# A state-space decoder layer with routed experts: router operands in PSUM, row norms on ScalarE, and evenly spread scatters and output matmuls

## The reference

```python
x = x + _L0_attn_ref(_layernorm(x, axis=-1), ...)     # state-space mixer
x = x + _L0_xattn_ref(_layernorm(x, axis=-1), ...)    # int8-quantised MLP, weights per sequence
x = x + _L0_ffn_ref(_layernorm(x, axis=-1), ...)      # 16 routed experts (top 2) and a shared one
```

```python
dA = jnp.exp(d_t[..., None] * A)
h = h * dA + (d_t * u_t)[..., None] * B_t[:, None, :]
y = jnp.einsum('bdn,bn->bd', h, C_t)
```

## Time and profile before

| | |
|---|---|
| median of 3 runs | 1877.12 us (1876.48 to 1877.83) |
| the profiled execution | 1878.76 us, its span in the trace 1876.7 us |
| busy: PE, VectorE, ScalarE, GpSimd | 1450.3, 1477.8, 762.5, 1057.5 us |
| first part, to the first scan | 0 to 118 us |
| scan stages of batch 0, 1, 2, 3 | 118 to 360, 487 to 777, 904 to 1192, 1319 to 1603 us |
| transitions | 360 to 487, 777 to 904, 1192 to 1319 us |
| `last` and the last stage | 1603 to 1680, 1680 to 1877 us |

### The profile page before, as it was taken

The page is one execution under the profiler, slowest core; times in us unless marked ns, Lnnn a source line. Parts: engine busy times, 40 slices in busy tenths (PEclk is TensorE's granted clock), DMA queues, the critical chain, the costliest instruction groups (busy, mean ns, idle before and its releaser), DMA issues.

```text
span 1876.7 us, 19131 instructions
## 1 busy us (share of the span) xinstructions
PE 1450.3 (77%) x5208; PEld 817.3 (44%) x5208; DVE 1477.8 (79%) x2381; ACT 762.5 (41%) x1296; POOL 1057.5 (56%) x643
## 2 busy tenths in 40 slices
PE   6926656998578899997669899996679998449872
PEld 2312212444344565443435565443445664237662
DVE  2269999787998999797989999788989998873111
ACT  3454344236423555237324555247324553021221
POOL 0079999403759889403859888305769987201001
PEclk9967778999689999998689999998779999768996
DMA  2360000413324674514324663624225773214884
GB/s 96 140 246 13 0 0 1 141 40 135 141 107 133 204 225 130 191 43 157 149 95 154 205 217 110 202 83 169 86 96 157 235 222 133 74 62 141 255 299 158
DMA packets 99019, 255.28 MB, mean 136 GB/s; under 512 B 11488, under 2 KB 11616, under 8 KB 93792
## 3 DMA queue, kind: packets, MB, share of 16 engines
q1 hardware_dynamic: 91680, 233.08, 37.3%
q0 software_dynamic: 5120, 16.78, 2.7%
q10 hardware_dynamic: 2112, 4.19, 0.6%
HBM read 211.02 MB, written 42.99 MB: 135 GB/s over the span
## 4 chain that ended last, share of the span: by engine, by line
PE 43%; DVE 25%; issue 17%; POOL 7%; DMA 4%; ACT 4%; SPq 1%; DVEq 0%; POOLq 0%; ACTq 0%
DVE bank L981 8%; PE bank L1578 7%; PE bank L1483 6%; PE bank L1695 5%; PE bank L1493 4%; POOL work L528 3%; PE bank L1524 3%; PE bank L1530 3%; PE bank L1531 3%; DMA ew_up<-in_exp_w 3%; DVE work L993 2%; PE bank L1602 2%; DVE pairs L993 2%; PE bank L1501 2%; PE bank L1594 2%
## 5 line engine op out<-in xcount | busy, mean ns | idle before, releaser
L528 POOL TENSOR_TENSOR work<-du,BB 128x1024 f32<-128x1024 f32 x256 | 603.5, 2363 | 4.6 <-DVE bank L981 4.2
L709 ACT ACTIVATE bank<-delta,A_sb 128x512 f32<-128x512 f32 x512 | 351.2, 690 | 622.1 <-DVE pairs L993 380.3
L981 DVE TENSOR_TENSOR_SCAN bank<-bank,work 128x512 f32<-128x512 f32 x448 | 543.0, 1219 | 22.7 <-POOL work L528 22.7
L1578 PEld LDWEIGHTS bank<-x3T,ew_up 128*128 128x128 f32 x1984 | 296.9, 198 | 132.0 <-issue 89.9
L1578 PE MATMUL bank<-x3T,ew_up 128*128 128x128 f32 (+1 forms) x1984 | 326.5, 312 | 35.6 <-DMA ew_up<-in_exp_w 21.7
L993 DVE TENSOR_TENSOR pairs<-bank,CB 128x512 f32<-128x512 f32 x256 | 172.5, 674 | 26.7 <-PE bank L1524 26.2
L556 POOL TENSOR_TENSOR work<-work 128x512 f32<-128x512 f32 x64 | 81.1, 1267 | 92.6 <-DVE work L993 92.6
L993 DVE TENSOR_TENSOR work<-bank,CB 128x512 f32<-128x512 f32 x192 | 128.7, 671 | 5.5 <-PE bank L1524 5.5
L1602 PE MATMUL bank<-ew_dn,etm 128*128 128x512 f32 x184 | 103.6, 646 | 32.4 <-ACT x3T L750 32.2
L488 POOL TENSOR_TENSOR col<-col,halfpow 128x4 f32<-128x4 f32 (+1 forms) x8 | 7.7, 965 | 213.9 <-DVE col L1106 213.9
L504 POOL TENSOR_TENSOR delta<-delta,work 128x512 f32<-128x512 f32 x32 | 51.0, 1622 | 133.6 <-ACT work L683 133.6
(11 more groups left out here) (181 smaller groups left out, 2312.4 us busy)
## 6 DMA issues: line engine op xcount, KB each, us to landing
ew_up<-in_exp_w SPq DMA_DIRECT2D x124, 512.0 KB, 3.8
ew_dn<-in_exp_w SPq DMA_DIRECT2D x124, 256.0 KB, 4.3
hm<-xs_dram SPq DMA_DIRECT2D x92, 256.0 KB, 4.6
ys_dram<-x3T SPq DMA_DIRECT2D x92, 256.0 KB, 4.5
wst<-in_w_in SPq DMA_DIRECT2D x64, 256.0 KB, 2.9
BB<-bc_dram SPq DMA_DIRECT2D x16, 1024.0 KB, 4.9
CB<-bc_dram SPq DMA_DIRECT2D x16, 1024.0 KB, 7.0
wst<-in_out_w SPq DMA_DIRECT2D x32, 256.0 KB, 4.7
```

The costliest lines, as they stand in the source:

```text
L528: nc.gpsimd.tensor_tensor(dBu[:, k % CHUNK_SLOTS, :, :], du[:, j % 2:j % 2 + 1, :].broadcast_to([P, 2, T]), BB[:, n0:n0 + 2, :], ALU.mult) ...
L709: nc.scalar.activation(R[q % RING][:, :], delta[:, j, :], ACT.Exp, scale=A_sb[:, j, n:n + 1]).then_inc(S["da_ready"], 1)
L981: V.tensor_tensor_scan(prod[c % (2 * PAIR_SLOTS)] if on_pool(c) else R[q % RING][:, :], R[q % RING][:, :], dBu[:, c // 2 % CHUNK_SLOTS, c ...
L1578: ins = mm(gu_bank(v)[:, part * n:(part + 1) * n], ew_up[:, q % UP_RING, part * D + k * P:part * D + (k + 1) * P], rhs, start=(k == 0), st ...
```

## The change

- The router's operands move. The logits are read where PE writes them (`lg`, bank 0). Counts, places and prefix sums lie in bank 3, the rest in the row buffer `hm`. The softmax isn't divided by its sum; the two weights, and the shared gate, are made from GpSimd sums (`gate_sums`, `gate_weights`) and two reciprocals on VectorE (`gates`, slot 22). Places follow in slots 10 and 11 instead of 16 to 19.
- The counts of the earlier token tiles come from PE: `rank` is 12 matmuls (24 instructions) at slot 9 instead of 2 (4) at slot 14. The first down projection, in bank 0 and bank 3, waits for `route_done` and moves from slot 11 to 12.
- The 8 scatters go one to a GpSimd slot, in slots 8 to 15. SyncE waits for the weights (GpSimd slot 17) before it loads rows to `hm`.
- Both row norms become ScalarE activations (`row_norm`) with scale and bias; GpSimd makes the bias with two small multiplies.
- The second residual is scaled within PSUM and added from there.
- The `softplus` multiply of blocks 0 to 3 moves to GpSimd (`softplus_lost`), behind the four sums.
- `D * u` is a matmul with a diagonal that ScalarE makes (`skip`), added into `Y`.
- The mixer's parts go one or two to a slot, slots 107 to 126 (`OUT_AT`), the heads' transposes share one bank (`HEAD_AT`), and the `x3` copies come before slot 0 on ScalarE.

```diff
+FIRST_DOWN_AT = 12
...
-ROUTE_PROB_AT = 8
-RANK_AT = 14
-RANK_VISIT = 3
-ROUTE_POS_AT = 16
-SCATTER_AT = 11
+ROUTE_TOP_AT = 7
+RANK_AT = 9
+PLACE_AT = 10
+GATE_SUMS_AT = 8
+GATES_AT = 22
+GATE_WEIGHTS_AT = 17
+SCATTER_AT = 8
+SKIP_AT = 10
 GATHER_AT = PAIRS + TAIL - 2
 COMBINE_AT = UNITS + TAIL - 2
 STATS_AT = 60
 NORM_AT = 66
-HEAD_AT = (104, 108, 109, 110)
-OUT_BANKS_AT = (111, 112, 115, 116)
-OUT_FIRST = 4
-OUT_AT = (117, 119, 121)
+HEAD_AT = (103, 105, 107, 109)
+OUT_AT = ((114, 107, 111, 116), (114, 108, 112, 117), (115, 109, 112, 118), (116, 110, 113, 118),
+          (119, 120, 120, 121), (122, 122, 123, 124), (124, 125, 126, 126))
...
+        lg = bank[0][:, 0:TT * (NE + 1)].rearrange("p (t e) -> p t e", t=TT)
+        ranks = bank[3][:, 0:TT * NE]
+        place = ranks.rearrange("p (t e) -> p t e", t=TT)
+        count = bank[3][:, 64:80]
+        tiles_in = [bank[3][:, 80 + NE * i:80 + NE * (i + 1)] for i in range(4)]
+        tef = bank[3][0:1, 144:144 + ROUTED]
+        posf = bank[3][:, 168:176].rearrange("p (i t) -> p i t", i=2)
+        topf = bank[3][:, 176:184].rearrange("p (i t) -> p i t", i=2)
+        def skip_diag(j):
+            return xT[:, 0, (j % 2) * P:(j % 2 + 1) * P] if j < NBLK - 2 else hm[:, 1, (j % 2) * P:(j % 2 + 1) * P]
...
+                sp.wait_ge(S["weights_ready"], 2 * (be + 1))
...
+                nc.gpsimd.tensor_tensor(row_shift[:], mv[:, :, 0], halfpow[:, 2, :], ALU.mult).then_inc(S["rstd_ready"], 1)
+                pool.wait_ge(S["rstd_ready"], 2 * (l + 1))
+                nc.gpsimd.tensor_tensor(row_shift[:], row_shift[:], rstd[:], ALU.mult).then_inc(S["row_shifted"], 1)
...
+            def softplus_lost(a, m):
+                pool.wait_ge(S["sp_lost"], NBLK * a + m + 1)
+                pool.wait_ge(S["sp_inv_ready"], NBLK * a + m + 1)
+                nc.gpsimd.tensor_tensor(sp_w[m % 4], sp_e[m % 4], sp_w[m % 4], ALU.mult).then_inc(S["sp_err_ready"], 1)
...
-                        softplus_less(a, i)
+                        softplus_lost(a, i)
+                    softplus_less(a, 0)
                     du_block(a, 0)
                     chunk(a, 0)
+                    for i in range(1, 4):
+                        softplus_less(a, i)
...
+                def gate_sums():
+                    pool.wait_ge(S["ex_ready"], b)
+                    pool.wait_ge(S["route_ready"], 2 * b)
+                    linkP.mark(nc.gpsimd.tensor_tensor(gm[:, 3, :], gm[:, 3, :], ones[:, 0:TT], ALU.add))
+                    linkP(nc.gpsimd.tensor_tensor(gm[:, 4, :], top[:, :, 0], top[:, :, 1], ALU.add))
+                    nc.gpsimd.tensor_tensor(gm[:, 3:5, :], gm[:, 3:5, :], gm[:, 3:5, :], ALU.add
+                                            ).then_inc(S["gate_sums"], 1)
+                def gate_weights():
+                    pool.wait_ge(S["gate_ready"], b)
+                    wait(pool, "mix_done", 2 * TT * (b - 1))
+                    for i in range(2):
+                        nc.gpsimd.tensor_tensor(tw[:, i, :], top[:, :, i], gm[:, 5, :], ALU.mult
+                                                ).then_inc(S["weights_ready"], 1)
...
-                                if k == SCATTER_AT + i:
+                                if k == SCATTER_AT + TT * i + t:
...
+                if a > 0 and t == 0:
+                    sc.wait_ge(S["nsum_done"], PAIRS * (a - 1) + NS // 2 * (NBLK - 2))
                 nc.scalar.copy(xT[:, :, t * P:(t + 1) * P],
-                               bank[t % 2][:, :].rearrange("p (k t) -> p k t", k=KD)).then_inc(S["xT_ready"], 1)
+                               bank[0][:, :].rearrange("p (k t) -> p k t", k=KD)).then_inc(S["xT_ready"], 1)
...
+                def skip(j):
+                    if j >= 2:
+                        sc.wait_ge(S["nsum_done"], PAIRS * b + NS // 2 * (j - 1))
+                    if j == NBLK - 2:
+                        wait(sc, "rows_ps", ROUTED * b)
+                        sc.wait_ge(S["bc_out"], 16 * (b + 1))
+                    nc.scalar.activation(skip_diag(j), ident[:], ACT.Identity, scale=dsk[:, j:j + 1]
+                                         ).then_inc(S["skip_ready"], 1)
...
+                if experts:
+                    for i in range(KD):
+                        x3(i)
...
-                            if p == i // 2:
-                                x3(i)
...
+            def row_norm(m, l):
+                src, dst = ((xn, x1n), (x2, xn))[l % 2]
+                sc.wait_ge(S["row_shifted"], l + 1)
+                for t in range(TT):
+                    nc.scalar.activation(dst[:, t, :], src[:, t, :], ACT.Identity, scale=rstd[:, t:t + 1],
+                                         bias=row_shift[:, t:t + 1]).then_inc(S["xn_ready"], 1)
...
+                row_norm(m, 2 * m)
...
+                row_norm(m, 2 * m + 1)
...
+                row_norm(m, 2 * m + 1)
...
-                    V.scalar_tensor_tensor(out=Y[:, :], in0=u[:, j, :], scalar=dsk[:, j:j + 1], in1=Y[:, :],
-                                           op0=ALU.mult, op1=ALU.add).then_inc(S["linkS"], 1)
-                    ve.wait_ge(S["linkS"], NBLK * b + j + 1)
...
-                            logits(b - 1, link)
-                        for step in range(7):
-                            if p == ROUTE_PROB_AT + step // 2:
-                                choice(b - 1, link, step)
-                        for step in range(8):
-                            if p == ROUTE_POS_AT + step // 2:
-                                places(b - 1, link, step)
+                            logits(b - 1)
+                        if p in (ROUTE_TOP_AT, ROUTE_TOP_AT + 1):
+                            top_two(b - 1, p - ROUTE_TOP_AT)
+                        if p in (PLACE_AT, PLACE_AT + 1):
+                            places(b - 1, p - PLACE_AT)
+                        if p == GATES_AT:
+                            gates(b - 1)
...
+                    ve.wait_ge(S["weights_ready"], 2 * (be + 1))
...
                         ve.wait_ge(S["wsc_ready"], self.r + 1)
                     ve.wait_ge(S["lin_ps"], TT * self.r + t + 1)
-                    V.scalar_tensor_tensor(out=x1n[:, t, :], in0=acc[t][:, :], scalar=rr[:, 1, t:t + 1], in1=wsc,
+                    V.scalar_tensor_tensor(out=dst, in0=acc[t][:, :], scalar=rr[:, 1, t:t + 1], in1=wsc,
...
-                    q.scaled(t, "linkO")
+                    q.scaled(t, acc[t][:, :], "linkO")
                 for t in range(TT):
                     ve.wait_ge(S["linkO"], link_o + TT + t + 1)
-                    V.tensor_tensor(x2[:, t, :], xn[:, t, :], x1n[:, t, :], ALU.add).then_inc(S["linkO"], 1)
+                    V.tensor_tensor(x2[:, t, :], acc[t][:, :], xn[:, t, :], ALU.add).then_inc(S["linkO"], 1)
...
                 ve.wait_ge(S["lg_ps"], b + 1)
-                link(V.tensor_copy(lg, bank[0][:, 0:TT * (NE + 1)].rearrange("p (t e) -> p t e", t=TT)))
-                link(V.tensor_reduce(gm[:, 0, :], lg[:, :, 0:NE], AX.X, ALU.max))
...
 
-            def choice(b, link, step):
...
+            def top_two(b, part):
...
-                    link.mark(V.tensor_reduce(gm[:, 1, :], pr[:, 0, :, :], AX.X, ALU.add))
-                    link.mark(V.tensor_scalar(gm[:, 3, :], gm[:, 3, :], 1.0, None, ALU.add))
...
                     carrier()
...
+                    linkG.wait()
                     carrier()
                     for t in range(TT):
...
+                    linkG.wait()
+                    linkG(V.tensor_copy(topf, topi[:, :, 0:2].rearrange("p t i -> p i t")))
                     for i in range(2):
...
-                            rows(topf[:, :, i]), ALU.is_equal))
-                        link.mark(V.scalar_tensor_tensor(out=tw[:, i, :], in0=top[:, :, i], scalar=0.5, in1=gm[:, 5, :],
-                                                         op0=ALU.mult, op1=ALU.mult))
-                    link.wait()
...
-                rank, count = ranks[:, 0, :, :], ranks[:, 1, :, :]
...
+                            rows(topf[:, i, :]), ALU.is_equal).then_inc(S["route_ready"], 1)
+            def gates(b):
+                ve.wait_ge(S["gate_sums"], b + 1)
+                linkG.mark(V.reciprocal(sg[:], gm[:, 3, :]))
+                V.reciprocal(gm[:, 5, :], gm[:, 4, :]).then_inc(S["gate_ready"], 1)
+                linkG.wait()
...
+                counts, up, tiles, sums = tiles_in
+                if part == 0:
                     ve.wait_ge(S["rank_ps"], b + 1)
...
+                    linkG.mark(V.memset(first_tile[:, 0:1], 0.0))
+                    linkG(V.tensor_scalar(counts, count, 1.0 / P, 0.5 - 0.5 / P, ALU.mult, ALU.add))
+                    linkG(V.tensor_scalar(up, counts, MAGIC, None, ALU.add))
+                    linkG(V.tensor_scalar(tiles, up, MAGIC, None, ALU.subtract))
+                    linkG(V.tensor_tensor_scan(sums, ones_row[:], tiles, 0.0, ALU.mult, ALU.add))
+                    linkG.mark(V.tensor_copy(first_tile[:, 1:NE + 1], sums))
```

(41 more changed lines are left out.)

150 lines of the change are left out of this document (43 added, 107 removed).

## The result

The changed kernel takes 1779.3 us (median of four runs, 1774.1 to 1785.6), against 1876.8 for the kernel before beside it: a ratio of 0.948, 95% interval 0.945 to 0.951. The prediction was 1790, with 1756 to 1830 as its range. The profiled execution took 1779.99 us, with a span of 1778.3.

The account below looks back on a forecast made before the run. VectorE and GpSimd bound the steady slots, router waits slots 1 to 32, PE the last slots and early transition. Three batches at -28, batch 0 at -6.5 and the last stage at +3 gave -87.5: 1790 us, range 1756 to 1830.

Parts of the forecast that it names:

- Router, -20: Slots 1 to 32 of each batch with experts: 85.91 us become 66, a gain of 20 (12 to 25).
- The rule on PSUM's fixed cost: Page against the router term: some 25 operations at 65 ns, 1.6 us a batch, total 5 us higher.
- D term, -3: Five blocks outside slots 1 to 32, VectorE rid of 0.75 us each: gain 3 a batch (0 to 3.75).
- that gap covers it: D term: PE, busy 25.48 of 29.63 us, has room for one more matmul of 0.88 a block.
- Mixer, -4: Last slots: five parts, 4.4 us, move ahead of slot 112 into PE's idle 4.15; gain 4 (1 to 6).
- Before the next scan, -4: End of transition: ScalarE's inverses start at 898.1 instead of 902.11, so products come 4 us earlier (-8 to +3).
- First norm, +3: After a scan: norm moves to ScalarE, last transposes end at 804.9, costing 3 us a batch (0.5 to 4).
- Last part, +3: Last stage: PE's rank instructions cost 2.6 us, its wait some 2, the row norm returns 2; +3 (0 to +8).
- PE does not become the bound in slots 12 to 36: Rival: PE needs 9.9 us against VectorE's 7.2 per four slots at clock 0.81; 1826 us, chance 0.17.
- GpSimd's queue does not set the start: Rival: slower GpSimd multiplies cancel the gain at the start and add 3 us; 1811 us, chance 0.10.
- The waits for GpSimd did not stay in the router: Rival: router waits stay since results go to SBUF, 13 of the 20 us not won; 1829 us, chance 0.04.
- no scatter waits over 0.17 behind the first: Rival: every scatter waits for its queue, not the eighth alone; at 5.36 us each, 1910 us, chance 0.04.

Follow-up runs that it names:

- d_dve: Changed kernel, but VectorE multiplies u by D and adds it to the finished block, without PE's extra matmul and ScalarE's diagonal: 1787.1 us.
- r_sbuf: Changed kernel, but VectorE's own router scratch is in the row buffer in SBUF again, while what PE writes stays in PSUM: 1799.8 us.
- mix_burst: Changed kernel, but with the mixer's parts in bursts at the slots of before: 1796.9 us.
- sc44: Changed kernel, but with four scatters in each of GpSimd's slots 8 and 9: 1803.4 us.
- start_old: Changed kernel, but softplus multiplies of blocks 0 to 3 and second row norm on VectorE, GpSimd's old order; second residual stays in PSUM: 1777.8 us.
- inv_first: Changed kernel, but ScalarE makes the inverses of blocks 4 to 7 ahead of the second row norm: 1775.5 us.
- best_di: Changed kernel, but first row norm on VectorE, D as matmul for blocks 0 to 5 only, inverses of blocks 4 to 7 before second norm: 1767.5 us.

## Why the prediction was right, point by point

- **Router, -20: shown, and 2.9 too small.** VectorE is busy 61.30 us where I had 62.2, and idle 1.76 where I had 4. The longest router operation takes 0.52 us. The place of the operands is worth 7.4 of the 22.9 and the spread scatters 7.4, each shown by undoing it alone. Of the other 8, 1.0 is the D term's (`d_dve`); what the fewer instructions and the counts on PE share of the rest was not taken apart. Another 2.5 came later and stood in no term: slots 32 to 47 took 33.56, with 2.17 of VectorE waiting for PE, and now take 31.07. They take 31.1 with D on VectorE or with the scratch in SBUF, and 31.5 with the scatters four and four, so none of these three gave it; what did stays open.
- **The rule on PSUM's fixed cost.** By the Trainium skill, VectorE: DVE Perf Modes, The TRN2 errata, I had estimated 65 ns more for each operation out of PSUM than for one out of SBUF. The same `tensor_scalar` of 16 columns took 0.17 in SBUF and 0.18 in PSUM, and the same copy into SBUF 0.18 out of SBUF and 0.17 out of PSUM (`r_sbuf` and the changed kernel): the trace does not show it.
- **D term, -3: right in size by luck, wrong in where.** I spread 0.75 over five blocks. Four of them gave 0.1 or nothing: in one GpSimd is full, in three VectorE waits for PE instead. One gave 3.4, by a wait for PE that I had not seen. PE's cover, "that gap covers it", failed in these three blocks, and again in the last two, whose matmuls cost 1.7 a batch. In batch 0 the term gained 2.8, as I had it (2.5), but 3.7 came on behind slot 112, so nothing was left.
- **Mixer, -4: shown at PE's first projection, -3.9.** Undoing it gave 5.7 there (`mix_burst`), and D's two matmuls take 1.7 of that back. What I said one would see, 34 to 35 us in the last 16 slots, was wrong: 28.55. Product buffers and the last sums let PE lag 9.1 us behind the last scan (743.58 less 734.48), where it was 3.1 behind before. The transition then looks 0.9 shorter, as I had said of it, but for two reasons that cancel: it starts with some 6 us of PE's work left, and its scans come earlier, ahead of the multiplies.
- **Before the next scan, -4: about the right size (-5.4), the wrong step.** I credited the norm on ScalarE and its earlier inverses and set VectorE's relief aside. Undoing the moves alone costs nothing, undoing the residual alone 0.7 to 1.7, undoing both 4.4 to 5.4.
- **First norm, +3: shown.** PE waits 1.97 and its transposes take 0.86 more, 2.8 in all; undoing it gave 3.0 in two transitions and 4.0 in the third.
- **Last part, +3:** 5, between the two profiles. It was not taken apart; it varies from 277 to 284 us over the profiles of the changed kernel and its variants, where the kernel before has 275.
- **The rivals.** PE does not become the bound in slots 12 to 36: VectorE waits for it 0.2 us in slots 1 to 32 and 0.7 in the next 16. It is near, since PE is busy 60.67 of the 63.06. The granted clock, 0.81 there before, is 0.94: PE idled 21.1 us of the stretch then and 2.4 now, so the low clock that the rival counted on is mostly gone. In `r_sbuf` PE idles 5.3 and the clock is 0.87, in `sc44` 8.5 and 0.89. GpSimd's queue does not set the start in the changed kernel (`start_old`), but it is what comes next (`inv_first`). The waits for GpSimd did not stay in the router, and in the three batches no scatter waits over 0.17 behind the first.

The sum was 11 us off, mostly by slots 1 to 47 (2.9 and 2.5 a batch), against a batch 0, a batch 2 and a last part that gave less.

## What to carry to other kernels

A small VectorE operation beside a busy GpSimd is priced by where its operands lie, not by its columns; here one operand in PSUM took the wait away from the cast and the comparison. A stage's gain is read at the engine that finishes it last: the last scan came 10 us earlier here, and PE 4. Where two edits relieve the same engine, undo each alone and both together before crediting one: here either would have done.

## What the runs showed of the hardware

The wait for GpSimd does not always end with the instruction that it began beside. In batch 2 of the changed kernel one instruction on four numbers a partition, all in SBUF, took 7.21 us; the rows of VectorE and GpSimd:

```profile
1003.42 7.21 DVE L998 SCALAR_TENSOR_TENSOR shift<-mv,rstd 128x4 f32<-128x4 f32 x1
```

```profile
1003.52 2.34 POOL L552 TENSOR_TENSOR work<-du,BB 128x1024 f32<-128x1024 f32 x1
1005.82 1.25 POOL L583 TENSOR_TENSOR pairs<-pairs 128x512 f32<-128x512 f32 x1
1007.04 2.34 POOL L552 TENSOR_TENSOR work<-du,BB 128x1024 f32<-128x1024 f32 x1
1009.35 1.25 POOL L542 TENSOR_TENSOR du<-delta,u 128x512 f32<-128x512 f32 x1
1011.94 2.36 POOL L552 TENSOR_TENSOR work<-du,BB 128x1024 f32<-128x1024 f32 x1 [1.34 <-DVE bank L1045]
```

Four GpSimd instructions followed one another, and VectorE's ended at 1010.63, with the last of them. GpSimd then idled 1.34 us, until VectorE's next scan: it had run out of work that did not need VectorE. The Trainium skill, SBUF — State Buffer, Who interferes with whom, lets whichever of VectorE and GpSimd issues first have a shared port pair for its whole instruction, while the other blocks, and counts VectorE operations with two SBUF inputs among those that need it when GpSimd's instruction reads SBUF. The trace agrees: in `r_sbuf` the comparison of `iota` with an SBUF tile waited, in the changed kernel, with a PSUM tile, it did not, and the searches for the largest, with one input, took their 0.17 beside a GpSimd multiply, as these rows of `r_sbuf` have it:

```profile
500.51 2.38 POOL L552 TENSOR_TENSOR work<-du,BB 128x1024 f32<-128x1024 f32 x1
500.87 0.17 DVE L1400 MAX8 hm<-hm 128x8 f32<-128x16 f32 x1
```

Two SBUF inputs are not the only case: the cast and the `tensor_scalar` of `r_sbuf` waited with one. That the loser can lose four turns running is what this run adds; `r_sbuf`, `mix_burst` and `best_di` each show the same 7.2 us once.
